# Second head group loaded in the first stage, splits moved to the chunk's end with two buffers, first group's maxima from chunk 7

## The chip, the cores and the metric

The kernel runs on one core of one Trainium2 chip. The metric is device time in microseconds, taken as the median of the runs of one program.

## The reference, cut to what matters

One transformer block over x of shape [4, 2048, 256]: a modulated layer norm, causal attention with 16 heads of 16 dimensions and rotary positions, a gated residual, a second modulated norm and a mixture of 16 experts (top 4) with a shared expert. The change lies in the attention's first part:

```python
h = layernorm(x) * (1 + ca) + sa
qkv = (h @ qkv_w + qkv_b).reshape(Bx, Tx, 3, H, HD).transpose(2, 0, 3, 1, 4)
q, k, v = (qkv[0], qkv[1], qkv[2])
q = _apply_rotary(q, rope)
k = _apply_rotary(k, rope)
scores = jnp.einsum('bhqd,bhkd->bhqk', q, k) * scale
scores = jnp.where(causal_mask, -jnp.inf, scores)
attn = jax.nn.softmax(scores, axis=-1)
out = jnp.einsum('bhqk,bhkd->bhqd', attn, v)
```

## The kernel before, in words

**Stages.** The first stage makes q, k and v. It walks over 16 chunks of 512 tokens (four chunks for each of the four sequences of the batch). Then comes the attention over 16 groups of four heads (four groups for each sequence, 40 steps of one key tile each), with the projection and the routing of finished parts beside it, and at last the experts. One list of items, written by `plan()`, sets the order; each engine walks the list and runs its part of every item, in that order and with semaphore waits. SyncE's queue (SP) issues nearly all transfers, in the same order.

**A chunk of the first stage.** `between(c, k)` is called at eight places of chunk c, k from 0 to 7; k = 0 to 3 lie in the half for q (z = 0), k = 4 to 7 in that for k (z = 1). A chunk holds these items:

- `rows` (L1387, DVE): the rows of the next chunk are scaled to `xn`, four operations, at k = 0. `turn` (L962, TensorE) transposes them to `hT` and waits for `xn`; its two halves stand at k = 1 and k = 3.
- `norm` (DVE, L1369 to L1374; GpSimd, L1711): the statistics of the chunk after the next, at k = 3.
- `qk` (L983), `v` (L994): the projections on TensorE. `rot` (L1420, L1423 on DVE, L1720 on GpSimd): the rotation, into `r`. `vb` (L1585, ACT): v from PSUM to `vst`, once in each half.
- `hi` and `lo` split a finished chunk `r` into three bf16 parts, which SP stores to DRAM (12 transfers). `hi`: ACT copies to bf16 (L1595), GpSimd subtracts (L1728, into `pe_`). `lo`: ACT copies the rest (L1599), and the last subtraction follows, on DVE (L1429) for chunks below 5 and above 13, on GpSimd (L1733) for the others. The parts stand in one of `PT_` buffers `pt`; `hi` waits on ACT until the buffer's last stores have landed.

**Maxima.** The softmax needs the maximum of each score row first. For each group 160 products (`max`, L1013, with L1016 and L1017 for the causal edge) go to one of two or three PSUM banks, and DVE reduces each (L1434). Group 0's maxima are spread over the first stage (`fill`), those of group g + 1 over the steps of group g, four in a step. Before they can run, the group's q and k are loaded from DRAM into one of three sets of `QO` and `KO` (`loadg`, 20 transfers, L787). Sets that are not yet needed hold the `pt` buffers in the first stage.

**Start of the attention.** The item `attend` makes each engine wait for what the stage must leave; SP waits for all stores of parts.

The tiles of the stage share one space, and two arenas in the unused sets of `QO` and `KO`.

Of the kernel before, what the change touches and what calls it, by code (L numbers as in the profile page):

```python
# [7 lines left out]
F32 = mybir.dt.float32  # L8
# [7 lines left out]
B, T, D, H, HD = 4, 2048, 256, 16, 16  # L16
# [13 lines left out]
BIG = 1e30  # L30
EPS = 1e-5

XT, PT_, NP, XI, YG, RB, XQ, YO, OS = 3, 3, 9, 5, 3, 8, 6, 3, 3
OWN = 5
STEPS = [(c, kt) for c in range(4) for kt in range(4 * c + 4)]
W_PARTS = ((0, 3), (3, 6), (6, 9), (9, 12), (12, 15), (15, NE))
# [6 lines left out]
NL = len(LOADS)  # L43
# [78 lines left out]
def plan():  # L122

    o, u = Order(), Units()
# [18 lines left out]
    early, filled = [], 0  # L143
    total = None
# [16 lines left out]
    def between(c, k):  # L161
        if c + 1 < 16:
            if k == 0:
                o("rows", c + 1)
                if c + 1 + XT < 16:
                    o("x", c + 1 + XT)
            if k == 1:
                o("turn", c + 1, 0)
            if k == 3 and c + 2 < 16:
                o("norm", c + 2)  # L170
            if k == 3:
                o("turn", c + 1, 1)
        if k == 0 and c > 0:
            o("hi", c - 1)
        if k == 4 and c > 1:
            o("lo", c - 2)

    def fill(c):
        nonlocal filled
        if c >= 8:  # L180
            filled += 1
            while len(early) > total - total * filled // 96:
                maximum(early.pop(0))

    for c in range(16):
        for z in (0, 1):
            for m in (2 * z, 2 * z + 1):
                for f in (0, 1):
                    o("qk", c, m, f)
                    fill(c)  # L190
                between(c, 4 * z + m % 2)
            for half in (0, 1):
                o("rot", c, z, half)
                if half == 0:
                    between(c, 4 * z + 2)
            for i in (2 * z, 2 * z + 1):
                o("v", c, i)
                fill(c)
            o("vb", c, z)
            between(c, 4 * z + 3)  # L200
        o("vstore", c)
        if c == 5:
            for part in range(NL):
                o("loadg", 0, part)
            o("loadv", 0)
            early.extend(max_items(0))
            total = len(early)
    o("hi", 15)
    o("lo", 14)
    o("lo", 15)  # L210
    while early:
        maximum(early.pop(0))
# [76 lines left out]

    part0 = chain(route(0), scatter(0))  # L290
    proj = [project(b) for b in range(4)]
    for part in range(NL):
        o("loadg", 1, part)
    mu = [item for g in range(1, 16) for item in max_items(g)]
    done = 0

# [17 lines left out]
    for n, (g, i) in enumerate(order):  # L314
        if i == 0:
# [4 lines left out]
                pumps.append([proj[g // 4], -8.0, 2])  # L320
            if g >= 8:
                pumps.append([part0, 0.0, 0.7 if g == 12 else 1.7 if g > 12 else 1.4])
        want = min(len(mu), max(160 * max(0, n - 10) // 26, 0) if n < 37 else 160 + 4 * (n - 36))
        quota = (want - done) // 2 * 2
        at = done
        ahead = order[n + 1] if n + 1 < len(order) else None
# [25 lines left out]
        part = (i - 12 if g == 0 else i - 4)  # L352
# [59 lines left out]
    for m in range(len(jobs) + 3):  # L412
# [10 lines left out]
        if m >= 3:  # L423
            n = m - 3 - sum(NI) - FIRST[1]
# [18 lines left out]
def program(nc, x, wqk, wv, bqk, bv, wo, ob, gw, gbias, w13, w2, cT, wmod, ropec, ropes, consts, fconst, out):  # L443
# [12 lines left out]
    o, u, jobs = plan()  # L456

    with ExitStack() as ctx:
        s = Sems(nc, ctx)
# [45 lines left out]
        qo_at = A.at  # L505
        QO = A("QO", [128, 3, 4, T], BF16)
        ko_at = A.at
# [6 lines left out]

        set2 = 2 * 4 * T * 2
        pools = [Arena(nc, nh_end, qo_at), Arena(nc, v_at + 16 * 68 * 4, int(nc.sbuf_usable_end))]
        late_pools = [Arena(nc, qo_at, qo_at + set2), Arena(nc, ko_at, ko_at + set2)]

        def A_(name, shape, dt, pools=pools):
            size = (int(np.prod(shape[1:])) * (2 if dt == BF16 else 4) + 31) // 32 * 32  # L520
            pool = next(p for p in [*pools, *late_pools] if p.at + size <= p.end)
            return pool(name, shape, dt)

        pt = [A_(f"pt{w}", [128, 3, 4, 512], BF16, late_pools) for w in range(PT_)]
        vst = A_("vst", [128, 2, 4, 4, 68], F32, late_pools)
        wm_s = A_("wm_s", [128, 2, 1536], F32)
        cT_s = A_("cT_s", [128, 2, 4], F32)
        ce = A_("ce", [128, 2, 4], F32)
        cd = A_("cd", [128, 2, 4], F32)
        cr = A_("cr", [128, 2, 4], F32)  # L530
        sc = A_("sc", [128, 2, 4], F32)
        cons = A_("cons", [128, 2, 128], F32)
        graw = A_("graw", [4, 4, 256], F32)
        gneg = A_("gneg", [4, 2, 256], F32)
        gsg = A_("gsg", [4, 2, 256], F32)
        wqk_s = A_("wqk_s", [128, 2, 512], F32)
# [1 line left out]
        bqk_s = A_("bqk_s", [128, 4], F32)  # L538
        bv_s = A_("bv_s", [128, 2], F32)
        bvB = A_("bvB", [128, 2, 128], F32)  # L540
        r = A_("r", [128, 2, 4, 512], F32)
        pe_ = A_("pe_", [128, 2, 4, 512], F32)
        rC = A_("rC", [128, T], F32)
        rS = A_("rS", [128, T], F32)
        xt = A_("xt", [128, XT, 4, 256], F32)
        xn = A_("xn", [128, 2, 4, 256], F32)
        hT = A_("hT", [128, 2, 2, 512], F32)
        ta = A_("ta", [128, 2, 512], F32)
        tb = A_("tb", [128, 2, 512], F32)
        st6 = A_("st6", [128, 2, 4, 6], F32)  # L550
        mv = A_("mv", [128, 2, 4, 2], F32)
        ve = A_("ve", [128, 2, 4], F32)
# [77 lines left out]
        for name, *at in o.items:  # L630
# [3 lines left out]
            if name == "lo":  # L634
                c = at[0]
# [17 lines left out]
            if name == "hs":  # L653
                p, t = at
                k = (TILES[0] * p + t) % 3
# [3 lines left out]
            if name == "scat":  # L659
                p, t, j = at  # L660
                k = hs_slot[p, t]
# [3 lines left out]
            if name == "jdown":  # L665
                kind, p, i = jobs[at[0]]
                k = at[0] % YO
# [1029 lines left out]
        def _(pool):  # L1697
            q = Once(pool)
# [5 lines left out]
            for name, *at in o.items:  # L1704
# [17 lines left out]
                elif name == "hi":  # L1722
                    (c,) = at
                    q.wait_ge(s["p_hi"], c + 1)
                    q.wait_ge(s["rsum"], 4 * c + 4)
                    if c >= 2:
                        q.wait_ge(*lo_done[c - 2])
                    pool.tensor_tensor(pe_[:, c % 2], r[:, c % 2], pt[c % PT_][:, 0], ALU.subtract).then_inc(s["p_rest"], 1)  # L1728
# [160 lines left out]
```

## Time and profile before

| | |
|---|---|
| median of 3 runs | 3373.62 us (3370.67 to 3384.54) |
| the profiled execution's own time | 3378.87 us |
| its span | 3377.1 us |
| busy, TensorE (PE) | 2970.4 us, 88% |
| busy, VectorE (DVE) | 2242.5 us, 66% |
| busy, ScalarE (ACT) | 1782.1 us, 53% |
| busy, GpSimd (POOL) | 1311.7 us, 39% |
| granted TensorE clock over the span | 0.939 of full |
| first stage | 0 to about 340 us |
| attention's group 0 | about 340 to 487 us |

An engine's share is an average over stages with different limits. The change touches the first 490 us, so what counts is which engine is waited for there. In a line of the timeline, the number in square brackets is how long the engine was idle before it and who ended that.

### The profile page before, as it was taken

To read this page: it belongs to the slowest core of one execution; us is meant where nothing else is said; L and a number is where in the kernel's file an instruction comes from. 1 tells how busy PE (TensorE), PEld (TensorE's weight loads), DVE (VectorE), ACT (ScalarE), POOL (GpSimd) and SP (SyncE) were. 2 spreads that over 40 slices of the span, in tenths; PEclk is the share of its full clock that TensorE was granted. 3 is DMA by queue.
4 is the path that set the end of the run, shared out by engine and by line. 5 is a ranking of instruction groups with operands and counts; after the bars stand their busy time and mean duration, and the time that the engine had idled before them with its cause. 6 is when DMAs were issued, how large, how long until landed. Compare 5 with 4: busy or idle time off the path is not lost.

```text
span 3377.1 us, 61010 instructions
## 1 busy us (share of the span) xinstructions
PE 2970.4 (88%) x22500; PEld 1632.5 (48%) x22500; DVE 2242.5 (66%) x5047; ACT 1782.1 (53%) x2736; POOL 1311.7 (39%) x1685
## 2 busy tenths in 40 slices
PE   7787799999999999999988878888877799999886
PEld 4433233334333333333333222227876788999775
DVE  7887498888788877999877756413821124655465
ACT  3322456665666655666544545664644465666322
POOL 6755112134322145211357446334045514441355
PEclk9988899999999999999989878998989899999998
DMA  4833512232222223122324332134355545564465
GB/s 162 209 99 101 116 33 57 62 79 63 68 60 63 60 57 92 43 38 61 76 87 127 93 97 84 51 126 143 91 161 166 163 124 167 179 182 143 143 178 150
DMA packets 290690, 359.05 MB, mean 106 GB/s; under 512 B 65404, under 2 KB 243212, under 8 KB 290140
## 3 DMA queue, kind: packets, MB, share of 16 engines
q1 hardware_dynamic: 259516, 279.94, 30.3%
q0 software_dynamic: 30208, 71.87, 7.0%
q8 instruction: 182, 2.98, 0.4%
q10 hardware_dynamic: 672, 3.34, 0.4%
q14 instruction: 112, 0.92, 0.1%
HBM read 206.25 MB, written 139.21 MB: 102 GB/s over the span
## 4 chain that ended last, share of the span: by engine, by line
PE 52%; DVE 12%; ACT 9%; issue 7%; POOL 3%; DMA 3%; SPq 3%; another core or an unknown queue 2%; POOLq 0%; ACTq 0%; DVEq 0%
PE PB L1139 12%; PE PB L1066 8%; PE PB L1155 8%; ACT P L1615 8%; DVE mx L1434 7%; PE PB L1013 6%; PE PB L1036 5%; PE PB L1049 5%; PE PB L1124 2%; PE PB L1080 2%; DMA ON<-osb 1%; SPq L844 1%; PE PB L1103 1%; POOL P L1762 1%
## 5 line engine op out<-in xcount | busy, mean ns | idle before, releaser
L1434 DVE TENSOR_REDUCE mx<-PB 128x1 f32<-128x512 f32 (+3 forms) x2560 | 1405.8, 603 | 293.1 <-PE PB L1013 155.5
L1615 ACT ACTIVATE P<-PB 128x1024 f32<-128x1024 f32 (+3 forms) x1280 | 1097.8, 894 | 791.9 <-PE PB L1049 771.7
L1013 PE MATMUL PB<-KO,QO 64*128 64x512 bf16 (+3 forms) x2560 | 782.2, 359 | 81.6 <-DVE mx L1434 56.5
L1066 PE MATMUL PB<-P,V 128*17 128x512 f32 (+3 forms) x5120 | 617.7, 555 | 15.6 <-POOL P L1762 15.6
L1036 PE MATMUL PB<-QO,KO 64*128 64x512 bf16 (+3 forms) x2560 | 550.7, 359 | 54.4 <-ACT P L1615 28.9
L1049 PE MATMUL PB<-QO,KO 34*128 34x512 bf16 (+3 forms) x2560 | 543.0, 359 | 42.7 <-remote 29.5
L1013 PEld LDWEIGHTS PB<-KO,QO 64*128 64x128 bf16 x2560 | 205.5, 94 | 769.7 <-DVE mx L1434 545.0
L1545 DVE TENSOR_TENSOR haT<-sl,PB 64x128 f32<-64x128 f32 x350 | 101.4, 290 | 556.7 <-ACT sl L1694 357.7
L1139 PE MATMUL PB<-xT,ws 128*128 128x128 f32 x3432 | 451.3, 284 | 19.3 <-issue 10.7
L1139 PEld LDWEIGHTS PB<-xT,ws 128*128 128x128 f32 x3432 | 425.1, 200 | 23.8 <-issue 13.0
L1762 POOL TENSOR_SCALAR_AFFINE_SELECT P<-P 128x256 f32<-128x256 f32 x512 | 205.3, 410 | 572.6 <-ACT P L1615 568.4
L1823 POOL DMA_INDIRECT yg<-y_slots,sidu x256 | 248.0, 969 | 401.5 <-DVE acc L1526 196.3
L1155 PE MATMUL PB<-W,haT 128*128 x1144 | 315.5, 400 | 57.8 <-issue 34.8
L1694 ACT ACTIVATE sl<-PB 128x256 f32<-128x256 f32 x350 | 134.1, 383 | 381.3 <-PE PB L1139 264.7
L1036 PEld LDWEIGHTS PB<-QO,KO 64*128 64x128 bf16 x2560 | 152.1, 95 | 239.0 <-ACT P L1615 198.3
L1049 PEld LDWEIGHTS PB<-QO,KO 34*128 34x128 bf16 x2560 | 191.2, 95 | 154.6 <-PE PB L1036 44.6
L1678 ACT ACTIVATE ws<-W 128x768 f32 x286 | 239.7, 838 | 23.0 <-issue 22.9
L1155 PEld LDWEIGHTS PB<-W,haT 128*128 128x128 f32 x1144 | 205.0, 200 | 84.1 <-issue 66.3
L1016 PE MATMUL PB<-tri,pick 64*128 64x128 bf16 x1024 | 219.2, 221 | 0.0
L1769 POOL TENSOR_TENSOR osb<-osb,rden 128x512 f32<-128x512 f32 x64 | 81.8, 1278 | 314.8 <-DMA rden<-rden_rows 307.1
L1810 POOL DMA_INDIRECT x_slots<-Rsg,sidu x172 | 166.4, 967 | 89.4 <-issue 47.3
L1017 PE MATMUL PB<-tri,pick 64*128 64x64 bf16 x1024 | 192.8, 193 | 0.0
(179 smaller groups left out, 3328.5 us busy)
## 6 DMA issues: line engine op xcount, KB each, us to landing
xq<-x_slots SPq DMA_DIRECT2D x286, 128.0 KB
qk_parts<-pt SPq DMA_DIRECT2D x192, 128.0 KB, 2.4
KO<-qk_parts SPq DMA_DIRECT2D x192, 128.0 KB, 3.8
y_slots<-yo SPq DMA_DIRECT2D x191, 128.0 KB
QO<-qk_parts SPq DMA_DIRECT2D x64, 256.0 KB, 3.6
rden<-rden_rows SPq DMA_DIRECT2D x256, 64.0 KB
y_slots<-mx SPq DMA_DIRECT2D x95, 128.0 KB
v_rows<-vst SPq DMA_DIRECT2D x16, 544.0 KB, 3.5
```

What stands on the lines that cost most here:

```text
L1013: mm = pe.matmul(PB[:, bank, 0:n], QO[half, k3, j, 128 * t:128 * t + 128], KO[half, k3, j, 512 * kc:512 * kc + n], start=True, stop=True)
L1016: pe.matmul(PB[:, bank, n - 128:n], pick[half, 0, :], tri[half, 0, :], start=False, stop=True, skip_group_check=True)
L1036: pe.matmul(PB[:, j, 0:n], KO[rows, k3, j, 128 * kt:128 * kt + 128], QO[rows, k3, j, q0:q0 + n], start=True, stop=False).then_inc(s["sa"], 1)
L1049: pe.matmul(PB[:, j, 0:n], KO[rows, k3, j, 128 * kt:128 * kt + 128], QO[rows, k3, j, q0:q0 + n], start=False, stop=True).then_inc(s["st"], 1)
L1066: mm = pe.matmul(PB[32 * j:32 * j + 17, 7, c0:512], V[:, g % 2, kt, 17 * j:17 * j + 17], P[:, pbuf(g, i, j // 2), j % 2, 0:n], start=kt == ...
L1139: mm = pe.matmul(PB[:, 2 + k, 128 * m:128 * m + 128], w[:, 128 * m:128 * m + 128], xT[:, k, f, :], start=f == 0, stop=f == 1)
L1155: mm = pe.matmul(PB[:, bank, 0:256], haT[:, k, f, :], w, start=f == 0, stop=f == 1)
L1434: dve.tensor_reduce(mx[:, j, t, kc:kc + 1], PB[:, u.bank[item], 0:n], AX.X, ALU.max).then_inc(s["mx"], 1)
L1615: act.activation(P[:, pbuf(g, i, p), :, 0:n], PB[:, 2 * p:2 * p + 2, 0:n], ACT.Exp, scale=0.25).then_inc(s["exp"], 1)
L1678: act.activation(ws[:, k], W13[:, :, bass.ds(of[p, i], 1), :].rearrange("p f o c -> p f (o c)"), ACT.Copy).then_inc(s["ws"], 1)
L1762: pool.affine_select(out=P[:, k, :, 0:128], in_=P[:, k, :, 0:128], compare_op=ALU.is_ge, fill=0.0, base=0, pattern=[[0, 2], [1, 128]], cha ...
L1823: pool.indirect_dma_start(yg[:, k, j, :], None, y_d[p][:, :], bass.IndirectOffsetOnAxis(sidu[:, i, j:j + 1], 0)).then_inc(s[f"l_yg{k}"], 16)
```

## The change

Seven things move; the arithmetic stays as it is.

1. `lo(c - 1)` stands at k = 7, the end of chunk c; before, `lo(c - 2)` stood at k = 4. `lo(14)` falls into chunk 15.
2. `PT_` is 2 where it was 3.
3. Group 0 is loaded after chunk 4, before after chunk 5.
4. Its 160 maxima are spread over the 108 places of chunks 7 to 15, before over the 96 of chunks 8 to 15.
5. Group 1 is loaded in the first stage, three or four transfers after each of the chunks 8 to 13; before, the 20 stood behind `attend`.
6. In the attention, 16 maxima of group 1 stand in step 0 and four in each later step; before, none stood in the first ten steps and about six in each of the 26 after them.
7. Tiles of the stage are laid out anew: `pt`, `ta` and `tb` leave one set of `QO` and `KO` free, and `pe_` takes the place of `wm_s` and `graw`, for which the first `hi` on GpSimd waits.

```diff
-XT, PT_, NP, XI, YG, RB, XQ, YO, OS = 3, 3, 9, 5, 3, 8, 6, 3, 3
+XT, PT_, NP, XI, YG, RB, XQ, YO, OS = 3, 2, 9, 5, 3, 8, 6, 3, 3
...
-        if k == 4 and c > 1:
-            o("lo", c - 2)
+        if k == 7 and c > 0:
+            o("lo", c - 1)
...
-        if c >= 8:
+        if c >= 7:
             filled += 1
-            while len(early) > total - total * filled // 96:
+            while len(early) > total - total * filled // 108:
                 maximum(early.pop(0))
...
-        if c == 5:
+        if c == 4:
             for part in range(NL):
                 o("loadg", 0, part)
             o("loadv", 0)
             early.extend(max_items(0))
             total = len(early)
+        if 8 <= c < 14:
+            for part in range((c - 8) * NL // 6, (c - 7) * NL // 6):
+                o("loadg", 1, part)
     o("hi", 15)
-    o("lo", 14)
     o("lo", 15)
...
-    for part in range(NL):
-        o("loadg", 1, part)
...
-        want = min(len(mu), max(160 * max(0, n - 10) // 26, 0) if n < 37 else 160 + 4 * (n - 36))
+        want = min(len(mu), 160 + 4 * (n - 36))
...
-        late_pools = [Arena(nc, qo_at, qo_at + set2), Arena(nc, ko_at, ko_at + set2)]
+        one = 4 * T * 2
+        late_pools = [Arena(nc, qo_at + one, qo_at + set2), Arena(nc, ko_at + one, ko_at + set2)]
...
+        pe_at = next(p.at for p in pools if p.at + 16384 <= p.end)
+        pe_ = A_("pe_", [128, 2, 4, 512], F32)
+        wm_s = nc.alloc_sbuf_tensor_at("wm_s", [128, 2, 1536], F32, offset=pe_at)
+        graw = nc.alloc_sbuf_tensor_at("graw", [4, 4, 256], F32, offset=pe_at + 12288)
...
                     q.wait_ge(s["rsum"], 4 * c + 4)
+                    q.wait_ge(s["m_gate"], 1)
+                    q.wait_ge(s["w_mod"], 16)
```

**Place 1, DVE in chunk 2.** Before, from the end of the statistics (`ve`) on; `ta` and `tb` are the rotation, `xn` the row scaling that opens chunk 3:

```order
L1374 TENSOR_SCALAR ve<-mv 128x4
L1429 TENSOR_TENSOR pt_100<-pe__120,pt_100 128x2048
L1420 SCALAR_TENSOR_TENSOR ta<-PB,bqk_s,rC 128x512
L1423 SCALAR_TENSOR_TENSOR tb<-PB,bqk_s,rS 128x512
L1420 SCALAR_TENSOR_TENSOR ta<-PB,bqk_s,rS 128x512
L1423 SCALAR_TENSOR_TENSOR tb<-PB,bqk_s,rC 128x512
L1387 TENSOR_SCALAR xn<-xt,mv,rstd 128x256 x4
```

The same place in the changed kernel, where lines are two further down:

```order
L1376 TENSOR_SCALAR ve<-mv 128x4
L1422 SCALAR_TENSOR_TENSOR ta<-PB,bqk_s,rC 128x512
L1425 SCALAR_TENSOR_TENSOR tb<-PB,bqk_s,rS 128x512
L1422 SCALAR_TENSOR_TENSOR ta<-PB,bqk_s,rS 128x512
L1425 SCALAR_TENSOR_TENSOR tb<-PB,bqk_s,rC 128x512
L1431 TENSOR_TENSOR pt_101<-pe__105,pt_101 128x2048
L1389 TENSOR_SCALAR xn<-xt,mv,rstd 128x256 x4
```

DVE's split subtraction has moved from between the statistics and the rotation to between the rotation and the next row scaling, and it is that of chunk 1 where it was that of chunk 0.

**Place 2, ACT at the end of an early chunk.** Before (`vst` is the copy of v, `hT` of the transposed rows, `pt<-pe_` the copy of `lo`, `pt<-r` that of `hi`):

```order
L1585 ACTIVATE vst<-PB 128x4x4x16 x2
L1576 ACTIVATE hT<-PB,mT 128x512
L1599 ACTIVATE pt_102<-pe__120 128x2048
L1585 ACTIVATE vst<-PB 128x4x4x16 x2
L1595 ACTIVATE pt_101<-r 128x2048
```

And in the changed kernel:

```order
L1587 ACTIVATE vst<-PB 128x4x4x16 x2
L1578 ACTIVATE hT<-PB,mT 128x512
L1587 ACTIVATE vst<-PB 128x4x4x16 x2
L1601 ACTIVATE pt_101<-pe__105 128x2048
L1597 ACTIVATE pt_100<-r 128x2048
```

The copy for `lo` now stands behind the chunk's second copy of v, right ahead of the copy for `hi`.

**Place 3, GpSimd around the end of a chunk with maxima.** Before (`rstd` belongs to the statistics, `pt<-pe_` is the subtraction of `lo`, `pe_<-r` that of `hi`):

```order
L1711 TENSOR_TENSOR rstd<-ve,mhalf 128x4
L1733 TENSOR_TENSOR pt_100<-pe__120,pt_100 128x2048
L1720 TENSOR_TENSOR r<-ta,tb 128x512 x2
L1728 TENSOR_TENSOR pe__120<-r,pt_102 128x2048
L1720 TENSOR_TENSOR r<-ta,tb 128x512 x2
```

And in the changed kernel:

```order
L1713 TENSOR_TENSOR rstd<-ve,mhalf 128x4
L1722 TENSOR_TENSOR r<-ta,tb 128x512 x2
L1737 TENSOR_TENSOR pt_100<-pe__105,pt_100 128x2048
L1732 TENSOR_TENSOR pe__105<-r,pt_101 128x2048
L1722 TENSOR_TENSOR r<-ta,tb 128x512 x2
```

The two long subtractions now follow one another, behind the chunk's last rotation and ahead of the next chunk's first.

## Rows read from the trace of the kernel before

**Rows 1.** The page, group of the maxima: count, busy us, mean ns

```profile
L1434 DVE TENSOR_REDUCE mx<-PB 128x1 f32<-128x512 f32 (+3 forms) x2560 | 1405.8, 603 | 293.1 <-PE PB L1013 155.5
```

**Rows 2.** Windows: span, then busy us (instructions) by engine, PEclk, DMA share, GB/s

```profile
340.80:370.00 29.20, 23.70 (x172) 5.46 (x172) 0.00 (x0) 18.46 (x24) 7.13 (x18) 0.82 0.68 153
370.00:383.60 13.60, 0.00 (x0) 0.00 (x0) 0.04 (x1) 0.00 (x0) 0.44 (x2) 0.57 1.04 159
```

**Rows 3.** Timeline (start, us, engine): last loads of the second group, TensorE's restart

```profile
368.11 0.89 SPq L787 DMA_DIRECT2D KO<-qk_parts  x2
383.67 0.30 PE L1013 MATMUL PB<-KO,QO 64*128 64x128 bf16 x2 [13.75 <-DMA KO<-qk_parts]
```

**Rows 4.** Timeline of ACT: copies of finished output chunks

```profile
486.86 0.60 ACT L1622 ACTIVATE osb<-PB 128x512 f32<-128x512 f32 x1
496.18 0.60 ACT L1622 ACTIVATE osb<-PB 128x512 f32<-128x512 f32 x1
587.83 0.60 ACT L1622 ACTIVATE osb<-PB 128x512 f32<-128x512 f32 x1
```

**Rows 5.** Timeline of chunk 6, first stage

```profile
107.51 2.85 DVE L1387 TENSOR_SCALAR xn<-xt,mv,rstd 128x256 f32<-128x256 f32 x4
116.00 3.05 DVE L1429 TENSOR_TENSOR pt<-pe__120,pt 128x2048 bf16<-128x2048 f32 x1 [0.30 <-ACT pt L1599]
118.44 0.66 ACT L1585 ACTIVATE vst<-PB 128x256 f32<-128x256 f32 x2 [2.48 <-PE PB L994]
120.95 0.73 DVE L1423 SCALAR_TENSOR_TENSOR tb<-PB,bqk_s,rC 128x512 f32<-128x512 f32 x1
121.61 2.85 DVE L1387 TENSOR_SCALAR xn<-xt,mv,rstd 128x256 f32<-128x256 f32 x4
124.51 0.66 PE L962 MATMUL PB<-ident,xn 128*128 128x128 f32 x4 [2.67 <-DVE xn L1387]
```

**Rows 6.** Timeline: chunk 3's parts stored, first group's first loads, first maximum

```profile
104.98 7.64 SPq L776 DMA_DIRECT2D qk_parts<-pt  x12
115.13 0.81 SPq L787 DMA_DIRECT2D QO<-qk_parts  x2
138.02 0.28 PE L1013 MATMUL PB<-KO,QO 64*128 64x128 bf16 x1 [4.67 <-DMA KO<-qk_parts]
```

**Rows 7.** Windows around a restart of TensorE

```profile
133.00:138.00 5.00, 0.36 (x1) 0.00 (x0) 0.82 (x2) 0.19 (x1) 5.00 (x3) 0.84 1.01 188
138.00:143.00 5.00, 4.98 (x15) 1.69 (x17) 2.21 (x7) 0.00 (x0) 1.66 (x2) 0.50 1.09 371
```

**Rows 8.** Timeline around the start of chunk 13

```profile
256.52 0.66 ACT L1585 ACTIVATE vst<-PB 128x256 f32<-128x256 f32 x2 [5.33 <-PE PB L994]
258.51 1.91 ACT L1595 ACTIVATE pt<-r 128x2048 bf16<-128x2048 f32 x1 [1.33 <-POOL r L1720]
260.50 4.06 POOL L1728 TENSOR_TENSOR pe__120<-r,pt 128x2048 f32<-128x2048 f32 x1 [2.02 <-ACT pt L1595]
264.38 1.38 DVE L1387 TENSOR_SCALAR xn<-xt,mv,rstd 128x256 f32<-128x256 f32 x4
```

**Rows 9.** GpSimd subtraction, row scaling by line (min/median/max), ends of value copies

```profile
162.97 4.06 POOL L1728 TENSOR_TENSOR pe__120<-r,pt 128x2048 f32<-128x2048 f32 x1 [2.02 <-ACT pt L1595]
L1387 DVE TENSOR_SCALAR xn<-xt,mv,rstd x4: 400/400/1909, 165.3 to 167.7; 128x256 f32<-128x256 f32 x4
159.00 0.66 ACT L1585 ACTIVATE vst<-PB 128x256 f32<-128x256 f32 x2 [6.03 <-PE PB L994]
184.40 0.66 ACT L1585 ACTIVATE vst<-PB 128x256 f32<-128x256 f32 x2 [6.59 <-PE PB L994]
232.85 0.66 ACT L1585 ACTIVATE vst<-PB 128x256 f32<-128x256 f32 x2 [5.62 <-PE PB L994]
```

**Rows 10.** The same at the end of the stage: GpSimd row, and line L1429

```profile
331.16 4.06 POOL L1728 TENSOR_TENSOR pe__120<-r,pt 128x2048 f32<-128x2048 f32 x1 [2.02 <-ACT pt L1595]
L1429 DVE TENSOR_TENSOR pt<-pe__120,pt x7: 2278/3048/4448, 58.9 to 337.3; 128x2048 bf16<-128x2048 f32 x7
```

More of the change, by code:

```diff
@@ L524, in program @@
         pt = [A_(f"pt{w}", [128, 3, 4, 512], BF16, late_pools) for w in range(PT_)]
-        vst = A_("vst", [128, 2, 4, 4, 68], F32, late_pools)
-        wm_s = A_("wm_s", [128, 2, 1536], F32)
+        ta = A_("ta", [128, 2, 512], F32, late_pools)
+        tb = A_("tb", [128, 2, 512], F32, late_pools)
+        r = A_("r", [128, 2, 4, 512], F32)
+        pe_at = next(p.at for p in pools if p.at + 16384 <= p.end)
+        pe_ = A_("pe_", [128, 2, 4, 512], F32)
+        wm_s = nc.alloc_sbuf_tensor_at("wm_s", [128, 2, 1536], F32, offset=pe_at)
+        graw = nc.alloc_sbuf_tensor_at("graw", [4, 4, 256], F32, offset=pe_at + 12288)
+        vst = A_("vst", [128, 2, 4, 4, 68], F32)
+        xt = A_("xt", [128, XT, 4, 256], F32)
+        xn = A_("xn", [128, 2, 4, 256], F32)
+        hT = A_("hT", [128, 2, 2, 512], F32)
+        rC = A_("rC", [128, T], F32)
+        rS = A_("rS", [128, T], F32)
         cT_s = A_("cT_s", [128, 2, 4], F32)
@@ L532, in program @@
         cons = A_("cons", [128, 2, 128], F32)
-        graw = A_("graw", [4, 4, 256], F32)
         gneg = A_("gneg", [4, 2, 256], F32)
@@ L540, in program @@
         bvB = A_("bvB", [128, 2, 128], F32)
[L541 to L549, printed above, removed]
         st6 = A_("st6", [128, 2, 4, 6], F32)
```

## The prediction

> **What bounds the kernel now.** I read the page first. It names TensorE the busiest engine, but the change touches only the first 490 us, so I went on to windows of that stretch, then to the timelines of its engines, one after the other.
>
> The largest hole is at the start of the attention. In the first ten steps TensorE is busy 23.70 of 29.20 us and DVE not at all; then for 13.60 us TensorE, DVE and ACT stand still [rows 2]. The row that ends this is the first maximum of group 1, after 13.75 us of waiting for the load of `KO`; the load's last two transfers were issued at 368.11 [rows 3]. They were late because SP had to issue the last 24 stores of parts and wait for their landing first.
>
> How fast a group can go is seen from the copies of finished output chunks on ACT: 486.86 ends group 0, 587.83 ends group 1, so a group with four maxima in each step takes 100.97 us; from its first such copy (496.18) to its last it is 91.65 us [rows 4]. Group 0 took 146.1 us, from TensorE's first product at 340.8, where the first window of [rows 2] begins, to 486.86.
>
> In the first stage, chunks 1 to 6 hold no maxima. There DVE sets the pace: from one row scaling at 107.51 to the next at 121.61 is 14.10 us, and it does not wait for more than 0.30 us in it; TensorE waits for the row scaling, 2.67 us [rows 5]. In chunks 8 to 15 TensorE and DVE hand the two banks of the maxima to each other; a chunk takes 23.67 us (from 232.85 to 256.52) [rows 8, 9].
>
> **Group 1 loaded early (parts 5 and 6).** The stall of 13.75 us goes for certain. More is won: the first ten steps had no maxima and left TensorE and DVE room, and the steps behind them had six each. With an even spread, group 0 from its first copy on should take what group 1 took, 91.65 us. The first copy comes after four steps, the pipeline's filling and 36 maxima (16 + 5 x 4). DVE needs 36 x 0.603 us = 21.7 us for these [rows 1], and TensorE starts them at the lower of its two clock levels (1.2 GHz), since it was idle before; I take 26.5 us, so group 0 takes 26.5 + 91.65 = 118.1 us where it took 146.1: **28 us saved**. From below: DVE's 21.7 us come whole behind some 8 us of filling, 25 us. From above: the first copy comes with the last of them, 33 us.
>
> **The split at the chunk's end, chunks 1 to 5 (parts 1 and 2).** The same operations run, but ahead of others. Take rows of chunk 6 as the pattern and call T the end of its row scaling, 107.51 + 2.85 = 110.36. The second copy of v ends at 118.44 + 0.66 = 119.10, T + 8.74; the rotation ends at 120.95 + 0.73, about T + 11.3 with the 3.05 us of split in it, so T + 8.3 without [rows 5]. Now ACT's copy for `lo` starts only behind the copy of v: T + 8.74 to T + 10.65 (1.91 us, the duration of its twin in [rows 8]). DVE stands from T + 8.3 to T + 10.65 and then subtracts, 2.28 us at the least [rows 10], to T + 12.93. ACT meanwhile copies for `hi`, to T + 12.56, so GpSimd's 4.06 us of subtraction is ready before DVE's row scaling is. Here the two get in each other's way. DVE's four row scalings take 400 ns each, but the one that began at 165.3 beside a GpSimd subtraction (162.97 + 4.06 = 167.03) took 1909 ns, until 167.2 [rows 9]. And the DVE subtraction that ran beside GpSimd's (331.16 to 335.22) took 4448 ns where the quickest took 2278 [rows 10]. So each waits until the other's running operation is over: GpSimd goes from T + 12.95 to T + 17.0, and the next T is about T + 18.3. A chunk takes 18.3 us, not 14.1: **5 x 4.2 = 21 us lost**, less about 1 in the first, so 20. If the two did not hinder each other the period would be 10.65 + 2.28 + about 1.6 = 14.5 and the loss some 2 us; with the row scaling at the 2.85 us that it took beside the short rotations it would be 15.8, 8 us. These are the lower ends.
>
> The Trainium skill states this as a rule (SBUF — State Buffer, section "Who interferes with whom"): DVE and GpSimd share one pair of SBUF ports, and for some forms "whoever issues first gets the shared pair for the whole instruction; the other fully blocks". By that rule a row scaling issued beside the 4.06 us subtraction waits for its whole rest, and the trace agrees: it ended 0.15 us behind it. It speaks against this change; were the port shared by halves, the loss would be the lower end.
>
> **The clock.** In each such chunk TensorE would be idle for about 2.67 + 4.2 = 6.9 us. What that does is shown at 138: after 4.67 us of idle the granted clock was 0.50 from 138 to 143 [rows 6, 7]. The projections behind T lie on the path. [...] **6 us lost.**
>
> **The first load (part 3).** It starts 10.15 us behind chunk 3's stores (104.98 to 115.13) and lands 22.9 us later, at 138.02, where TensorE had waited 4.67 us [rows 6]. In the changed kernel the stores stand half a chunk earlier, some 8 us, and are delayed by three chunks' 4.2 us and the first wait: they begin at about 110, and the load lands at about 143. Chunk 6 ends at 121.7 + 20, about 142. The wait of 4.67 us mostly goes: **4 us won**. Two buffers make `hi(6)` wait for chunk 4's stores, some 3 us on ACT, hidden while the load is awaited.
>
> **Maxima over nine chunks (part 4).** The number is the same; chunk 7's own work is now interleaved. Nothing by itself (a fill costs what it cost): 0.
>
> **Chunks 7 to 14.** GpSimd's two subtractions now come one after the other. Around the start of chunk 13: the copy of v ends at 257.18, ACT's copy for `lo` would end at 259.1, GpSimd would subtract to 263.2 and, for `hi`, to 267.3. The row scaling is issued at 264.38 [rows 8] and would wait 2.9 us for it. Before, it met the last 0.2 us of the subtraction or nothing. Does such a delay reach the end of the chunk? Chunk 9's row scaling lost 1.5 us this way and the chunk took 25.40 us (159.00 to 184.40) against 23.67 [rows 9]: all of it, as far as one chunk tells. I take 2.5 us in seven chunks, **17.5 us lost**; bounds 1.2 us (DVE's idle share takes up the rest) and 3.3 us each (the row scaling is issued 0.4 us sooner, with fewer maxima ahead of it), 8 and 23. More idle of TensorE may bring more of the lower clock: 0 to 12 us, **3 taken**.
>
> **The end of the stage.** ACT copies for `lo(14)` first, and DVE's subtraction then lies ahead of GpSimd's last one, which waits for it: **2 us lost**. The waits on `m_gate` and `w_mod` were met long before: 0. The 20 transfers of group 1 in the stage, 0.45 us of SP each [rows 3], lie where SP waits anyway: 0.
>
> **Sum.** -28 + 20 + 6 - 4 + 17.5 + 3 + 2 = +16.5 us. The profiled execution took 3378.87 us, so 3395.4; it lay 5.25 us above the median, so **3390 us** against 3373.62.
>
> **The cases.** What a measurement of this kernel can tell from no change is about 0.5%, 16.9 us, so below 3356.7 and above 3390.5 count.
>
> - *My forecast* (0.50): the first stage gives back more than the attention wins; net +8 to +25, 3382 to 3399.
> - *The blocks are mostly hidden* (0.20): in the chunks with maxima, DVE's idle share takes up the delay and the clock does not fall: 20 + 8 + 2 - 4 - 28 = -2, 3372. For it: DVE waits for TensorE in these chunks, and TensorE for DVE, so a delay need not add up. Against it: chunk 9.
> - *Faster* (0.17): the order of DVE and GpSimd at the chunk's end falls the other way, so that the row scaling gets in ahead of the subtraction. Then the early chunks lose 8 us or less and the later ones little: 8 + 5 + 1 - 4 - 28 = -18, 3355. It decides from the point where the row scaling is issued before ACT's copy for `hi` is over, T + 12.56 in my working, and I have it at T + 12.93: 0.4 us. For it: this small margin. Against it: the copy's start moves with the same events as DVE's.
> - *The clock takes more* (0.13): TensorE falls to the lower level in most chunks of the stage: 8.5 + 12 in place of 6 + 3, and 23 for the blocks: +33, 3407.
>
> That group 1's load would still be waited for I leave at nothing: its last transfers stand behind chunk 13, two chunks ahead of use.
>
> The range that leaves no more than 2 in 10 outside is 3360 to 3408. Faster by over 0.5%: 0.18; within: 0.40; slower: 0.42, all of the dear case and rather more than half of the forecast's upper part.
>
> **What would show it.** No wait of TensorE for `KO` near the attention's start; group 0 about 119 us long. DVE idle for about 2.3 us ahead of L1431 in chunks 1 to 5, and the period of their row scalings 18 us or more; a first row scaling of 3 to 4 us beside GpSimd in these chunks, and one of about 3 us in chunks 8 to 14. The attention beginning 40 to 48 us later than at 340. If the row scalings stay at their 1.4 us for four, the blocking is wrong and the kernel is faster; if the attention begins before 365 us, the forecast fails to the fast side.

## The result and the profile after

The changed kernel takes **3396.53 us** in the median (3386.38 to 3406.75, 14 runs). The kernel before, run beside it on the same chip, takes 3371.51 us (3359.77 to 3384.54, 14 runs). The ratio is 1.0073, 95% interval 1.0059 to 1.0086: slower by 25 us. The forecast was 3390 us, slower by 16.5.

| | before | after |
|---|---|---|
| span of the profiled execution | 3377.1 us | 3392.3 us |
| mean granted TensorE clock | 0.939 | 0.935 |
| start of the attention | 340.8 | 397.9 |
| last output chunk of group 0 copied | 486.9 | 510.1 |
| from the one to the other | 146.1 us | 112.2 us |

**The attention.** The windows of the same length as in [rows 2], counted from its new start (columns as there):

```profile
397.90:427.10 29.20, 27.22 (x222) 11.07 (x224) 23.46 (x46) 14.68 (x18) 5.12 (x13) 0.78 0.33 95
427.10:440.70 13.60, 13.04 (x130) 4.72 (x127) 12.87 (x24) 9.31 (x13) 4.07 (x8) 1.00 0.14 44
```

DVE now works 23.46 us where it had nothing to do, and the stretch in which all stood still is gone. Here are ACT's first and last copies of group 0's finished chunks; the last answers to the first row of [rows 4]:

```profile
418.44 0.60 ACT L1624 ACTIVATE osb<-PB 128x512 f32<-128x512 f32 x1
...
510.10 0.60 ACT L1624 ACTIVATE osb<-PB 128x512 f32<-128x512 f32 x1
```

20.5 us to the first copy, 91.66 us from it to the last: 112.2 us, 33.9 us less than before.

**Chunks 1 to 5.** The timeline of the end of chunk 5, with only the rows that carry the period; it answers to [rows 5]. The row scaling before this one ended at 118.87, which is T here:

```profile
118.93 1.11 PE L964 MATMUL PB<-ident,xn 128*128 128x128 f32 x4 [6.47 <-DVE xn L1389]
...
129.05 0.74 DVE L1425 SCALAR_TENSOR_TENSOR tb<-PB,bqk_s,rC 128x512 f32<-128x512 f32 x1
...
129.99 1.91 ACT L1601 ACTIVATE pt<-pe__105 128x2048 bf16<-128x2048 f32 x1
...
131.79 1.91 ACT L1597 ACTIVATE pt<-r 128x2048 bf16<-128x2048 f32 x1
...
131.94 2.29 DVE L1431 TENSOR_TENSOR pt<-pe__105,pt 128x2048 bf16<-128x2048 f32 x1 [2.15 <-ACT pt L1601]
...
133.78 4.36 POOL L1732 TENSOR_TENSOR pe__105<-r,pt 128x2048 f32<-128x2048 f32 x1 [2.64 <-ACT pt L1597]
...
134.15 5.12 DVE L1389 TENSOR_SCALAR xn<-xt,mv,rstd 128x256 f32<-128x256 f32 x4
```

Read downward, T being the end of a row scaling: the rotation ends at T + 10.9, DVE waits 2.15 us for ACT's copy, subtracts for 2.29, and its row scaling then takes 5.12 us, until 1.1 us behind the end of GpSimd's subtraction (138.14). The period is 20.4 us here and 19.8 to 20.4 in chunks 2 to 5, where it was 13.6 to 15.3. (Chunk 1 takes 15.6 us from row scaling to row scaling, where it took 11.6.) TensorE stands for 6.47 us, and what that does to its clock is in the windows behind T of chunks 3 and 4:

```profile
78.50:82.00 3.50, 3.50 (x11) 2.96 (x12) 3.50 (x8) 0.78 (x1) 2.14 (x2) 0.50 0.71 197
...
98.50:102.00 3.50, 3.38 (x10) 2.91 (x11) 3.50 (x8) 0.78 (x1) 1.99 (x2) 0.50 0.71 199
```

The granted clock is at its lower level, 0.50 of full; in the kernel before it is 1.00 in the 3.5 us behind T (82.2 to 85.7, 96.3 to 99.8).

**The first load.** TensorE's wait of 4.67 us in [rows 6] is gone. The first maximum of group 0 follows the projection without a pause:

```profile
149.68 1.02 PE L985 MATMUL PB<-hT,wqk_s 128*128 128x512 f32 x2
150.64 0.23 PE L1015 MATMUL PB<-KO,QO 64*128 64x128 bf16 x1
```

**Chunks with maxima.** GpSimd's two subtractions and DVE's row scaling in chunk 8, then in chunk 7; they answer to [rows 8]:

```profile
178.39 4.07 POOL L1737 TENSOR_TENSOR pt<-pe__105,pt 128x2048 bf16<-128x2048 f32 x1 [0.29 <-ACT pt L1601]
182.42 4.11 POOL L1732 TENSOR_TENSOR pe__105<-r,pt 128x2048 f32<-128x2048 f32 x1
180.85 6.47 DVE L1389 TENSOR_SCALAR xn<-xt,mv,rstd 128x256 f32<-128x256 f32 x4
...
152.41 4.07 POOL L1737 TENSOR_TENSOR pt<-pe__105,pt 128x2048 bf16<-128x2048 f32 x1 [0.84 <-ACT pt L1601]
156.44 4.10 POOL L1732 TENSOR_TENSOR pe__105<-r,pt 128x2048 f32<-128x2048 f32 x1
152.49 8.85 DVE L1389 TENSOR_SCALAR xn<-xt,mv,rstd 128x256 f32<-128x256 f32 x4
```

The row scaling is four operations of 0.40 us. Issued 0.1 us behind the start of the first subtraction it ends 0.8 us behind the second: the group was held through both. Taken one by one, the first operation takes 4.14 us and ends 0.15 us behind the first subtraction; the second takes 4.14 us again and ends 0.15 us behind the second one. In chunks 7 to 14 it takes 8.85, 6.47, 5.20, 5.26, 4.48, 6.88, 6.70 and 5.84 us, where before it took 1.36 to 2.88.

**The balance in the profiled executions.** Chunk 6's rotation ended at 121.7 and ends at 150.2: +28.5. From there to the start of the stage's last copies of v 205.2 us became 232.4: +27.2. From that to the attention's first product 13.9 became 15.3: +1.5. Sum +57.1, less 33.9 in group 0: +23.2 us, near the 25 of the medians. (The spans of the two profiled executions differ by 15.2 only: behind group 0, where the change touches nothing, that of the changed kernel took 8 us less.)

### The profile page after: what moved, and what is told of

Read it like the earlier page. It is cut to its first block, busy times and chain, and to the rows that moved or that the text cites. A ratio compares the mean times of both kernels' runs of the same rounds, so it can differ in the third digit from the quotient of the medians.

```text
span 3392.3 us, 61011 instructions
## 1 busy us (share of the span) xinstructions
PE 2965.1 (87%) x22500; PEld 1638.3 (48%) x22500; DVE 2281.4 (67%) x5047; ACT 1780.1 (52%) x2736; POOL 1302.6 (38%) x1685
## 4 chain that ended last, share of the span: by engine, by line
PE 51%; DVE 10%; ACT 10%; issue 6%; another core or an unknown queue 4%; POOL 3%; DMA 3%; SPq 2%; ACTq 0%; DVEq 0%; POOLq 0%
PE PB L1141 12%; ACT P L1617 9%; PE PB L1157 8%; PE PB L1068 8%; DVE mx L1436 6%; PE PB L1015 6%; PE PB L1038 5%; PE PB L1051 5%; PE PB L1126 2%; PE PB L1082 2%; DMA ON<-osb 1%; SPq L846 1%; DMA rden_rows<-r 1%; PE PB L1105 1%
## 5 line engine op out<-in xcount | busy, mean ns | idle before, releaser
L1051 PE MATMUL PB<-QO,KO 34*128 34x512 bf16 (+3 forms) x2560 | 535.5, 358 | 40.5 <-remote 31.0
L1141 PEld LDWEIGHTS PB<-xT,ws 128*128 128x128 f32 x3432 | 424.6, 199 | 18.8 <-ACT xT L1687 14.1
```

The costliest lines, as they stand in the source:

```text
L1051: pe.matmul(PB[:, j, 0:n], KO[rows, k3, j, 128 * kt:128 * kt + 128], QO[rows, k3, j, q0:q0 + n], start=False, stop=True).then_inc(s["st"], 1)
L1141: mm = pe.matmul(PB[:, 2 + k, 128 * m:128 * m + 128], w[:, 128 * m:128 * m + 128], xT[:, k, f, :], start=f == 0, stop=f == 1)
```

## Experiments

The edits are to the changed kernel, but for one to the kernel before. A ratio is to the kernel before on the same chip. Chips differ: the kernel before takes 3155.5 us on that of the first four runs, 3395.4 on that of the next four and 3156.05 on that of the last four.

**1. The third split at the seventh place.** Theory (P): the order at the chunk's end is the whole loss, since DVE and GpSimd hold each other off there.

```diff
-        if k == 7 and c > 0:
+        if k == 6 and c > 0:
             o("lo", c - 1)
```

> The changed kernel with one edit: lo(c - 1) stands at k = 6, between the two halves of the rotation, and no longer at k = 7. Two buffers, the early load of group 1 and all else stay. Theory P (the order at the chunk's end: ACT's copy behind that of v, and GpSimd's long subtractions ahead of DVE's row scaling): the early chunks come back to about 14.5 us, those with maxima to about 22.6, no row scaling over 2 us, and the attention starts at about 345; 34 us stay won in group 0, so about 3340 us, 1% faster than before. Rival B (two buffers: hi waits for stores on ACT): buffers are unchanged, so the stage stays at about 398 us and the time at 3395. Rival C (TensorE's clock by itself): it follows the idle time, so it goes the way of P and is not told apart here.

3119.49 us, ratio **0.9887** (0.9867 to 0.9907). One place earlier turns a loss of 0.7% into a gain of 1.1%. The early period is 13.8 us, shorter than before's 14.1, with row scalings of 2.32 us; the attention starts near 342.6, and group 0 takes 112 us as in the changed kernel. The two buffers, the early loads and the new layout are all in it, so none of them is the loss. One thing was not as expected: not all row scalings are under 2 us, that of chunk 10 takes 5.20. GpSimd's rows at the start of chunk 9, and the row scaling:

```profile
167.67 4.06 POOL L1737 TENSOR_TENSOR pt<-pe__105,pt 128x2048 bf16<-128x2048 f32 x1
171.69 1.26 POOL L1722 TENSOR_TENSOR r<-ta,tb 128x512 f32<-128x512 f32 x1
174.97 4.08 POOL L1732 TENSOR_TENSOR pe__105<-r,pt 128x2048 f32<-128x2048 f32 x1 [2.02 <-ACT pt L1597]
...
172.11 1.96 DVE L1389 TENSOR_SCALAR xn<-xt,mv,rstd 128x256 f32<-128x256 f32 x4
```

The row scaling lies between the two subtractions.

**2 and 3. One half of the chunks each.** Run 2 has the end (k = 7) for the chunks where DVE subtracts and the seventh place (k = 6) for the others; run 3 has it the other way round.

```diff
+        if k == (7 if c - 1 < OWN else 6) and c > 0:   # run 2
+        if k == (6 if c - 1 < OWN else 7) and c > 0:   # run 3
```

> The changed kernel with lo(c - 1) at k = 7 only for the five chunks whose last subtraction runs on DVE (0 to 4), at k = 6 for the others. Theory P: the early chunks stay at about 20.1 us (28 us lost against before), the chunks with maxima come back to 22.6 us; about 3396 - 30 = 3366 us. Rival B: no change from the changed kernel, 3395.

> The reverse: k = 6 for chunks 0 to 4, k = 7 for the others, whose two subtractions then follow one another on GpSimd. Theory P: early chunks about 14.5 us, chunks with maxima about 26.5 us with a first row scaling of over 3 us in each; about 3396 - 28 = 3368 us. Rival B: 3395.

Run 2: 3150.61 us, 0.9981 (0.9968 to 0.9995), as expected. Run 3: 3153.59 us, 0.9994 (0.9982 to 1.0005), near the 0.998 that was expected. Against run 1 the end costs 31 us in the early chunks and 34 in the later ones, 65 together. The changed kernel's ratio lies 0.0186 above that of run 1 (1.0073 against 0.9887), which is 59 us on this chip: within the intervals the two losses add up. The row scalings follow the place of the third: in the early chunks they take 5.11 us in run 2 and 2.31 in run 3, and those that take 4.2 to 6.9 us from chunk 8 on are run 3's.

**4. GpSimd's subtraction for `hi` cut short**, to 128 of 2048 columns, in chunks 2 to 15. This kernel leaves that much of the split out.

```diff
-                    pool.tensor_tensor(pe_[:, c % 2], r[:, c % 2], pt[c % PT_][:, 0], ALU.subtract)...
+                    pool.tensor_tensor(pe_[:, c % 2, 0, 0:128], r[:, c % 2, 0, 0:128], pt[c % PT_][:, 0, 0, 0:128], ALU.subtract)...
```

> The changed kernel, with GpSimd's subtraction for hi cut to 128 of 2048 columns for chunks 2 to 15; it leaves that much of the split out, so k and q are less exact. The order stays. Theory P with the port: nothing long runs on GpSimd when DVE's row scaling is issued, which takes 0.4 us each again; early chunks 15 us instead of 20.1 (DVE's wait for ACT's copy of 2.15 us stays), chunks with maxima 22.6; about 3345 to 3352 us. Rival to the port (what costs is DVE's wait for ACT's copy and the clock): the row scalings of 5.1 us stay long, and no more than 5 us are won.

3127.92 us, 0.9922 (0.9901 to 0.9942), as expected. The order is untouched, only the length of the operation on the other engine. In chunk 3:

```profile
86.34 2.29 DVE L1431 TENSOR_TENSOR pt<-pe__105,pt 128x2048 bf16<-128x2048 f32 x1 [2.15 <-ACT pt L1601]
88.55 1.49 DVE L1389 TENSOR_SCALAR xn<-xt,mv,rstd 128x256 f32<-128x256 f32 x4
```

DVE's wait of 2.15 us is still there, the row scaling is down from 5.12 to 1.49 us, and the period from 20.1 to 14.3. So nearly all of the early loss is the block, directly and through TensorE's clock, and the wait for ACT by itself costs close to nothing. This is the cleanest evidence for P.

The same trace prices the clock. These are the 5 us behind T in three chunks, one behind the other:

```profile
75.80:80.80 5.00, 4.97 (x22) 3.52 (x23) 4.86 (x14) 2.10 (x4) 2.93 (x3) 1.00 0.73 203
90.10:95.10 5.00, 5.00 (x18) 4.00 (x19) 4.44 (x13) 2.10 (x4) 2.95 (x3) 0.66 0.73 203
106.00:111.00 5.00, 4.97 (x22) 3.52 (x23) 4.86 (x14) 2.11 (x4) 2.93 (x3) 1.00 0.73 203
```

The row scaling takes 1.49 us in all three. With the clock at 1.00 the rotation ends at T + 8.4 and the period is 14.3 us; with 0.66 it ends at T + 10.1 and the period is 15.9. In the changed kernel, where the clock is 0.50 in the first 3.5 us behind T, the rotation ends at T + 10.4 to 10.9.

The chunks with maxima come back too: from the end of chunk 6's rotation to the last copies of v it is 207.5 us, against 232.4 in the changed kernel and 205.2 before.

**5. The changed kernel again, on the chip of runs 6 to 8.**

> The changed kernel itself, as the control on the chip of the following runs. Ratio to before about 1.007, attention starting at about 398 us of the span, group 0 about 112 us long. All theories expect the same.

3417.07 us, 1.0063 (1.0039 to 1.0086): the result holds on a second chip.

**6. The moved third and two buffers alone**, in the kernel before.

```diff
-XT, PT_, NP, XI, YG, RB, XQ, YO, OS = 3, 3, 9, 5, 3, 8, 6, 3, 3
+XT, PT_, NP, XI, YG, RB, XQ, YO, OS = 3, 2, 9, 5, 3, 8, 6, 3, 3
...
-        if k == 4 and c > 1:
-            o("lo", c - 2)
+        if k == 7 and c > 0:
+            o("lo", c - 1)
...
-    o("lo", 14)
     o("lo", 15)
```

> The kernel before with parts 1 and 2 alone: lo(c - 1) at k = 7, two buffers; loads and maxima as before. Theory P: the first stage loses what it lost in the changed kernel, about 28 us in the early chunks and some 5 us in each of the chunks with maxima but the last, and nothing is won behind it: 1.016 to 1.02 of before (55 to 65 us slower); the 13.75 us wait for the load of group 1 stays. If the loss came from the loads brought into the stage or from starting the maxima a chunk sooner (rival D), this kernel would be near 1.00.

3431.06 us, 1.0090 (1.0059 to 1.0121): a miss, it should have been 1.016 to 1.02. The early chunks are as expected (row scalings of 5.11 us). The later ones are not: 2.33, 1.66, 5.18, 3.96, 4.33, 1.36, 3.85 and 4.14 us. And the wait for `KO` is 7.4 us, not 13.75; that chunk 14's parts are stored sooner is the likely reason, which no run parts from others. Something in the changed kernel makes the later blocks longer than the moved third alone does; run 12 asks what.

**7. The old spread of group 1's maxima.**

```diff
-        want = min(len(mu), 160 + 4 * (n - 36))
+        want = min(len(mu), max(160 * max(0, n - 10) // 26, 0) if n < 37 else 160 + 4 * (n - 36))
```

> The changed kernel with the old spread of group 1's maxima: none in the attention's first ten steps, about six a step behind. Group 1 is still loaded in the first stage. It parts the 34 us won in group 0: the stall on the load is 13.75 us, so group 0 should take about 146 - 14 = 132 us less 1 or 2 for the lower clock behind the stall, and the even spread is worth the other 18 to 20 us. So about 18 us slower than the changed kernel, 1.0125 of before. If the load was all (rival), it is as fast as the changed kernel.

3438.89 us, 1.0110 (1.0077 to 1.0143), 22 us above the changed kernel on the same chip (run 5), where 18 were expected. Group 0 takes 131.1 us, as expected. Of the 33.9 us won in group 0, 15.0 come from the load (146.1 to 131.1) and 18.9 from the even spread: a part that looks like bookkeeping is worth more than the stall that is easy to see.

**8. The third right behind the row scaling.** `lo(c - 2)` at k = 0 of chunk c, so that the row scaling is always first.

```diff
-        if k == 7 and c > 0:
-            o("lo", c - 1)
+        if k == 0 and c > 1:
+            o("lo", c - 2)
```

(The loads of group 0 follow `lo(3)` in chunk 5, and `lo(14)` stands at the stage's end.)

> The changed kernel with lo(c - 2) at k = 0 of chunk c, directly behind the row scaling (so that DVE does its row scaling first), and group 0's load behind chunk 3's stores in chunk 5. On DVE the split still comes behind ACT's copies and beside GpSimd's subtraction; only the row scaling is ahead of both. Theory P: the early chunks take about 14 to 15.5 us and the row scalings in them about 2.8 us; GpSimd's two subtractions still follow one another in the later chunks, so those stay at about 26.5 us: 28 us faster than the changed kernel, about 0.999 of before. If the wait for ACT's copy is the cost and not the row scaling's, the early chunks stay at 18 us or more.

3397.04 us, 1.0000 (0.9975 to 1.0025), about as expected. The early period is 12.89 us, the shortest of all orders (run 9 has it too). The later chunks take 23.5 to 29.4 us, 26.5 on average, since there GpSimd still does both subtractions around the row scaling (6.46 us in chunk 8).

**9 and 10. The same with the fifth place for GpSimd's chunks.** Run 9 joins run 8's early chunks, its loads of group 0 included, with `lo(c - 1)` at k = 4 later; run 10 has k = 6 early and k = 4 later.

```diff
+        if k == 4 and c > OWN:                         # run 9
+            o("lo", c - 1)
+        if k == 0 and 1 < c < OWN + 2:
+            o("lo", c - 2)
...
+        if k == (6 if c - 1 < OWN else 4) and c > 0:   # run 10
```

> The changed kernel with the last third of a chunk placed by the engine that subtracts it: where VectorE subtracts (the first five chunks) it stands right behind the next but one chunk's row scaling, as in the run with rows first, and where GpSimd subtracts it stands after the fifth step of the next chunk, not at its end. Theory (the end of a chunk is the bad place, since there a subtraction of GpSimd lies beside VectorE's row scaling): early period 12.9 us as in the rows-first run, and between chunks 7 and 14 row scalings of 1.4 to 3.3 us where the changed kernel has 4.5 to 8.9; ratio 0.984 to 0.989, below both kernels. Rival (two buffers of the split are the price): the subtraction at the fifth step waits for GpSimd's first one, chunks of 26 us stay, ratio near 1.000. Rival (clock): the stage shortens, and the granted clock takes half of it back, ratio 0.992.

> The changed kernel with the last third at the seventh step of the next chunk where VectorE subtracts and at the fifth where GpSimd does. Theory: early period 13.8 us as in the first run, no row scaling over 3.5 us in the later chunks, ratio 0.985 to 0.989. Against the run with the seventh step everywhere (0.9887) it tells what the fifth step brings GpSimd's chunks: nothing or up to 4 us, the one row scaling of 5.2 us there. Rival (two buffers): a wait of ScalarE for the first subtraction at the fifth step holds the turned tiles behind it, ratio above 0.991.

3133.74 us, 0.9924 (0.9911 to 0.9936), and 3132.33 us, 0.9920 (0.9906 to 0.9933): both beat both kernels, both miss what was expected, and run 1 stays the best. Both ratios are those that a rival had named, but its mechanism is not in the traces. For run 9 the rival had the stage shorter and the clock taking half of it back; the attention starts at 358.9, later than the 340.8 before. For run 10 it had ACT waiting for GpSimd's subtraction; the only such wait of its copy for `lo` in the chunks with maxima is 1.1 us. I had taken "not at the end" for the rule. It is not enough. At the start of chunk 9 of run 10 GpSimd and DVE have

```profile
166.55 4.06 POOL L1737 TENSOR_TENSOR pt<-pe__105,pt 128x2048 bf16<-128x2048 f32 x1
171.33 2.58 POOL L1722 TENSOR_TENSOR r<-ta,tb 128x512 f32<-128x512 f32 x2 [0.71 <-DVE tb L1425]
175.93 4.06 POOL L1732 TENSOR_TENSOR pe__105<-r,pt 128x2048 f32<-128x2048 f32 x1 [2.02 <-ACT pt L1597]
...
176.99 4.12 DVE L1389 TENSOR_SCALAR xn<-xt,mv,rstd 128x256 f32<-128x256 f32 x4
```

and the row scaling is issued 1.1 us into the second subtraction. In run 1 the last third splits the rotation's two additions and so delays the second subtraction until the row scaling is through. The row scalings of chunks 7 to 14 add up to 22.8 us in run 10 and to about 19 in run 1; that is 4 us of the 10 or so between them. From chunk 7's row scaling to chunk 14's the granted clock is 0.93 in run 10 and 0.95 in run 1; how much of the rest that is stays open.

**11. Run 1 with the loads of group 0 after chunk 5 and its maxima from chunk 8.**

```diff
-        if c >= 7:
+        if c >= 8:
             filled += 1
-            while len(early) > total - total * filled // 108:
+            while len(early) > total - total * filled // 96:
...
-        if c == 4:
+        if c == 5:
             for part in range(NL):
```

> The run with the seventh step everywhere (0.9887), and with it the loads of group 0 after chunk 5 and its maxima from chunk 8, as before the change. Theory (the placement of the third is the whole loss, the earlier load and the spread of the maxima are worth nothing by themselves): 0.987 to 0.991. Rival (the earlier load gives or costs something by itself): a difference of over 0.003 from 0.9887 either way; with ten more us of maxima packed into eight chunks instead of nine nothing else moves.

3132.27 us in the median of six executions (3123.73 to 3142.96), ratio 0.9930 (0.9911 to 0.9949). A seventh, the profiled one, took 6103.65 us; it is left out, and its trace isn't used. The ratio is 0.0043 above run 1, so the theory missed and the rival was right. With the third well placed, the earlier load and the wider spread are worth some 14 us together, as far as two ratios from two chips with these intervals tell.

**12. The changed kernel with the same edit.** The third stays at k = 7.

> The changed kernel (third at the chunk's end) with the loads of group 0 after chunk 5 and its maxima from chunk 8. It tells why the run with only the third moved lost less in the later chunks (11 to 15 us) than the changed kernel (about 30). Theory: with 20 maxima in a chunk where the changed kernel has 18, and none in chunk 7, VectorE comes to the row scaling later, when GpSimd's first subtraction is partly over, so it meets one subtraction more often than two: row scalings of 1.4 to 5.2 us between chunks 7 and 14, ratio 1.002 to 1.004 (some 12 us under the changed kernel). Rival (the loads of group 1 inside these chunks make the difference): row scalings as in the changed kernel, 4.5 to 8.9 us, ratio 1.006 to 1.009.

3162.93 us, 1.0023 (1.0013 to 1.0032), as expected: 0.005 or 16 us **below** the changed kernel's 1.0073, and 13 us below its 1.0063 in run 5. Here is the start of chunk 9, GpSimd and DVE:

```profile
189.43 4.06 POOL L1737 TENSOR_TENSOR pt<-pe__105,pt 128x2048 bf16<-128x2048 f32 x1 [0.57 <-ACT pt L1601]
193.45 4.06 POOL L1732 TENSOR_TENSOR pe__105<-r,pt 128x2048 f32<-128x2048 f32 x1
...
193.56 1.29 DVE L1436 TENSOR_REDUCE mx<-PB 128x1 f32<-128x512 f32 x2 [1.12 <-PE PB L1015]
194.77 3.86 DVE L1389 TENSOR_SCALAR xn<-xt,mv,rstd 128x256 f32<-128x256 f32 x4
```

The row scaling comes 5.3 us behind the start of the first subtraction and meets only the second; in the changed kernel's chunk 9 it comes 3.7 us behind (208.76 against 205.04) and meets both. From the end of the last copy of v to the row scaling (means over chunks 9 to 14) it is 6.8 us here, 6.9 us in the kernel before, and 5.2 us in the changed kernel, where the second subtraction starts about 5.9 us behind that copy. With 160 maxima in 108 places a chunk has 18 where it had 20, and between that copy and the row scaling DVE has six reductions where it had seven. It is not the load, which this run moves as well: run 8 loads group 0 in chunk 5 too, but has six reductions there and a mean of 5.3 us, while run 6 has seven and 6.8. So DVE comes to the row scaling sooner in the changed kernel, and the first subtraction is still running in all of chunks 7 to 14 but chunk 11 (in chunk 10 for its last 0.1 us). The row scalings of chunks 7 to 14 add up to 49.7 us in the changed kernel, 26.7 here and 14.3 before: 23 us less here, of which 13 to 16 show in the time. The same edit costs some 14 us with the third at k = 6 and brings 13 to 16 with it at k = 7.

## Why the prediction was right, and where it was off

- **The case.** The forecast case came: the first stage gives back more than the attention wins. The measured median lies in the range, 6.5 us above the value, and its +25 is the upper edge of the case's +8 to +25. Slower by over 0.5% had 0.42 against 0.40 for no change; the measurement is on that side.
- **Attention, -28.** Measured -33.9, just beyond the upper end of 33. The stretch from the first copy on was right (91.66 against 91.65). Too long was the lead: 20.5 us where I had 26.5. I had added to DVE's 21.7 us for 36 maxima; in the trace only 33 reductions stand ahead of the first copy, with more of the shorter forms among them (18.5 us added up), and DVE is idle for only 4.4 us in that stretch, whatever the lower clock (0.78 over the first 29.2 us) adds included.
- **Chunks 1 to 5, +20, and their clock, +6.** Together 26, measured 28.5. The wait of DVE (2.15 us), the subtraction and a row scaling of 5.12 us came as worked out. The period is 20.2 us on average and not 18.3, since the rotation ends at T + 10.7, not T + 8.3: TensorE runs its projections at the lower clock after 6.47 us of idle. Run 4 bears this out, with T + 8.4 in a chunk at full clock and T + 10.1 in one at 0.66, and shows that both hang on the block. So the clock's part is about 2.4 us in a chunk. No row or run shows the 6 us that I took for it, 1.2 a chunk, nor the 8.5 us of the dear case. Part of it was made good by the rest of the period, which is about 0.5 us shorter than worked out.
- **The port rule.** A row scaling issued beside a GpSimd subtraction waits for its end: 5.12 us here against 1.49 in run 4, where the subtraction is short. The Trainium skill's rule (SBUF — State Buffer, section "Who interferes with whom") is borne out, and so is its statement there that `tensor_reduce` on trn2 never contends: two maxima beside the subtraction at 193.45 in run 12, which read PSUM, take 1.29 us.
- **First load, -4.** TensorE's wait of 4.67 us is gone: -4.7.
- **Chunks with maxima, +17.5 and +3.** This is the step that was mis-sized. +27.2 with the load's -4.7 in it, so about 32 us where I had 20.5. I took the row scaling to be issued at its old distance behind the copy of v (7.2 us, 264.38 against 257.18 in [rows 8]), so that it met the second subtraction alone, and allowed 0.4 us for fewer maxima. It is issued 3.9 to 6.8 us behind in chunks 8 to 14 (4.3 in chunk 8, 180.85 against 176.52) and 1.95 us in chunk 7, and meets both subtractions in seven of the eight chunks. Chunk 7, where the row scaling takes 8.85 us, had no term of its own. The time of the row scalings grew by 35 us (49.7 against 14.3), nearly all of which reached the end of the stage. Run 12 restores the old count of maxima in a chunk, and with it the distance of 6.8 us; each row scaling then meets one subtraction at most. Run 4, with the subtraction for `hi` short, brings the stretch back to within 2.3 us of before. What the clock takes of the 32 us was not separated.
- **End of the stage, +2.** Measured +1.5.
- **The rival on the faster side** needed the row scaling ahead of GpSimd's subtraction. Its margin was 0.4 us in my working; in the trace GpSimd's row starts 0.37 us ahead of DVE's (133.78, 134.15), and in chunk 1 only 0.08 us (53.41, 53.49). It did not happen in any of the five chunks, but the mechanism is real: run 8 forces this order, and the early period falls to 12.89 us.
- **The signs.** DVE's wait, the period of 18 us or more and the vanished wait for `KO` came. The attention began 57.1 us later, beyond the 40 to 48 that I had named, and group 0 took 112 us and not 119.
- **The balance.** 11.4 us too little in the chunks with maxima and 2.5 in the early ones, less 5.9 too little won in the attention, 0.7 at the load and 0.5 at the stage's end: 6.8 us, which is the difference of 23.2 from 16.5 but for rounding. One term missed by more than the result did, and the attention's miss hid half of it. The direction follows from the mechanism; that the value came within 6.5 us is in part luck.

Shown by a run: that the place of the third is the loss (1), that it splits into the two halves (2, 3), that the length of GpSimd's operation carries it (4), the two shares in group 0 (7), that the maxima ahead of the row scaling decide how many subtractions it meets (12, with 6 and 8), and, in the early chunks, what the clock takes (4). Not separated: the clock's share in the chunks with maxima, and all that parts run 10 from run 1.

## What to carry to other kernels

Before moving an operation of DVE or GpSimd, write down when the other engine's long operations start, and where DVE's short ones on the critical path fall between them: here one place out of eight was worth 1.9% of the kernel, in both halves of a stage. Count what stands ahead of the short operation too, since one reduction fewer ahead of it, free by itself, moved it from one blocking operation into two. Free the stall and spread the work into it: the even spread was worth more than the stall.

## What the runs showed of the hardware

A row scaling of four 0.40 us operations is held through two GpSimd operations one behind the other, 8.85 us in all (chunk 7). One of the four comes through between them: the first ends 0.15 us behind GpSimd's first operation, and the second, 4.14 us long, 0.15 us behind GpSimd's second. Where the row scaling's record begins only 0.13 us before the end of GpSimd's first operation (chunk 10, 236.17), none does: its first operation takes 4.30 us, until 0.15 us behind GpSimd's second. (DVE's records overlap the one before by about 0.08 us, so which of the two engines was ready first can't be told there.)

GpSimd is held too, by less: its subtraction takes 4.06 us alone, 4.36 beside the end of DVE's subtraction (133.78), and 4.92 at the end of the stage (387.41), where DVE's subtraction ran from 386.14 to 388.42.

The kernel before takes 3371.5, 3395.4 and 3155.5 us on three of the chips used here, up to 7.6% apart, and the changed kernel's ratio is 1.0073 and 1.0063 on the first two. So times were compared on one chip only.
